# Attention and experts on one core: norms moved to ACT, bulk loads to ACT's queue, score matmuls in pairs, keys by batch

## The reference

```
x = x + attention(layernorm(x), context)     16 heads of 16, distance bias per head
x = x + experts(layernorm(x))                top 2 of 8 experts, 256 -> 1024 (gelu) -> 256
scores = q k^T / 4 - slope[h] * |key - query + 870|;  attn = softmax(scores);  out = (attn v) Wo + bo
combine = top-2 of softmax(x Wg + bg), scaled to sum 1;  y = sum_e combine[e] * (gelu(x W1[e] + b1[e]) W2[e] + b2[e])
```

## Time and profile before

| | us |
|---|---|
| median of 3 runs | 512.09 (512.02 to 512.95) |
| the profiled execution | 508.91 |
| its span | 507.1 |
| TensorE busy | 419.6 (83%) |
| VectorE busy | 312.6 (62%) |
| ACT busy | 232.4 (46%) |
| GpSimd busy | 223.7 (44%) |
| mean granted TensorE clock | 0.922 |

### The profile page before, as it was taken

One profiled execution on the slowest core, in us unless ns is written; L12 is line 12 of the kernel. 1 busy time (PEld: TensorE's weight loads), 2 busy tenths in 40 slices (PEclk: granted clock), 3 DMA queues, 4 the chain that ended last, 5 costly groups with the idle time before them and its releaser, 6 DMA issues. The chain is left out here.

```text
span 507.1 us, 16158 instructions
## 1 busy us (share of the span) xinstructions
PE 419.6 (83%) x5137; PEld 330.3 (65%) x5138; DVE 312.6 (62%) x875; ACT 232.4 (46%) x607; POOL 223.7 (44%) x305
## 2 busy tenths in 40 slices
PE   5565768897888999995179899989989998999981
PEld 2554556676666778873168677668867876777760
DVE  5357848796778777554526466636664765566560
ACT  1333636564555564563234444534543553445430
POOL 3123528887888886677602222222222232122232
PEclk9865979898989999998579999989998999999997
DMA  6574455555646535333322223113222322122110
GB/s 225 134 229 150 139 152 189 175 175 192 215 136 185 165 123 163 122 123 127 127 64 37 39 41 53 35 29 45 46 44 31 53 38 43 34 43 47 22 12 0
DMA packets 52967, 50.70 MB, mean 100 GB/s; under 512 B 22672, under 2 KB 47024, under 8 KB 52784
## 3 DMA queue, kind: packets, MB, share of 16 engines
q1 hardware_dynamic: 45192, 41.07, 27.0%
q0 software_dynamic: 7152, 8.47, 9.9%
q10 hardware_dynamic: 576, 0.53, 0.3%
HBM read 33.73 MB, written 17.50 MB: 101 GB/s over the span
## 5 line engine op out<-in xcount | busy, mean ns | idle before, releaser
L976 PE MATMUL ps<-area,wts 128*128 128x128 f16 (+1 forms) x2896 | 197.0, 243 | 0.1
L976 PEld LDWEIGHTS ps<-area,wts 128*128 (+1 forms) x2896 | 157.5, 103 | 41.0 <-issue 2.1
L976 PE MATMUL ps<-wts,area 128*128 x624 | 153.4, 330 | 2.2 <-DVE area L934 1.8
L718 ACT ACTIVATE area<-ps,late 128x128 f32<-128x128 f32 x312 | 89.2, 368 | 115.0 <-PE ps L976 115.0
L932 DVE TENSOR_SCALAR area<-area 128x512 f16<-128x512 f32 x78 | 33.0, 424 | 77.8 <-ACT area L718 77.7
L976 PE MATMUL ps<-area 128*128 128x154 f16 (+2 forms) x928 | 71.0, 236 | 12.0 <-DMA area<-qd 11.1
L976 PEld LDWEIGHTS ps<-area 128*128 128x128 f16 (+1 forms) x928 | 59.8, 107 | 21.2 <-issue 8.1
L595 POOL DMA_INDIRECT out<-o,row_id x20 | 31.6, 1579 | 95.1 <-issue 65.0
L595 POOL DMA_INDIRECT out<-xn,row_id x19 | 30.0, 1579 | 92.4 <-issue 79.8
L804 DVE TENSOR_REDUCE mx<-ps 128x3 f32<-128x462 f32 (+1 forms) x96 | 53.1, 579 | 24.3 <-PE ps L976 23.9
L621 ACT ACTIVATE area<-ps 128x512 f32<-128x512 f32 x80 | 47.3, 595 | 27.7 <-PE ps L976 25.5
(11 more groups left out here) (121 smaller groups left out, 419.1 us busy)
## 6 DMA issues: line engine op xcount, KB each, us to landing
stage<-in_w SPq DMA_DIRECT2D x32, 512.0 KB, 5.0
area<-xlist SPq DMA_DIRECT2D x39, 130.0 KB, 2.0
area<-qd SPq DMA_DIRECT2D x16, 256.0 KB, 2.7
qd<-wts SPq DMA_DIRECT2D x48, 64.0 KB, 1.9
area<-in_x SPq DMA_DIRECT2D x16, 128.0 KB, 2.3
out<-area SPq DMA_DIRECT2D x16, 128.0 KB, 1.8
xlist<-pad_rows SPq DMA_DIRECT2D x11, 130.0 KB, 2.5
area<-in_b SPq DMA_DIRECT2D x1, 1024.0 KB, 5.0
```

The lines of the kernel that those rows point to most:

```text
L718: last = nc.scalar.activation(h32[par][:, c * P:(c + 1) * P], h_ps[par][m][:, f * P:(f + 1) * P], ACT.Gelu_apprx_tanh, bias=b1T[:, ds(e * ...
L976: return nc.tensor.matmul(out_, lhsT, rhs, start=start, stop=stop, skip_group_check=skip)
```

## The change

- POOL keeps the power and gets a tiny `shift` = -mean/std. The norms themselves become one ACT instruction each, x * scale + bias. `normed2` moves from the end of turn b1 to the next turn, behind ACT's copies of xn^T and o_sb; `normed1` stands near the end of ACT's turn.
- `load_w`, `late` and the kink tables are issued by ACT, the weights at the end of its turn, and two small writes of the keys' bias rows too.
- Scores: the heads are taken in natural order, so that the two heads of a pair share one weight load and one matmul of 314 columns where both lie in one group: ten matmuls a tile instead of sixteen. The kink tiles' extra matmuls stay.
- Keys are loaded, projected, split and written batch by batch. In turns -2 and -1 the next query stands ahead of the scores. `values()` moves from turn -3 to turn -2, behind the first scores.
- One bias matmul of two rows instead of two of one. From turn 16 on VectorE's weight splits stand at the end of the turn.

The diff, cut ("..." marks what is left out):

```diff
-GROUPS = [(0, 3), (3, 3), (6, 3), (9, 3), (12, 2), (14, 2)]
+GROUPS = [(0, 3), (3, 3), (6, 2), (8, 3), (11, 3), (14, 2)]
...
-            def load_w(u):
...
                 sp.dma_start(qs[R_MAX:R_MAX + 65:64, t % 4, :, :].rearrange("p n (j t) -> p n j t", j=4), src).then_inc(S[f"m_in{t % 4}"], 16)
 
+            sp.dma_start(a_sb[:, 0:A_ONE], pack_a[:, 0:A_ONE]).then_inc(s.a_in0, 16)
             load_x(0)
-            sp.dma_start(a_sb, pack_a).then_inc(s.a_in, 16)
             sp.dma_start(c32[:], c32_in).then_inc(s.c_in, 16)
...
             for b in range(B):
+                sp.wait_ge(s.k_hi, b + 1)
+                for a in (0, 1):
+                    sp.dma_start(parts[:, a, :, b], k16[:, b, 0]).then_inc(S[f"kd_w{b}"], 16)
+                sp.wait_ge(s.k_lo, b + 1)
+                sp.dma_start(parts[:, 2, :, b], k16[:, b, 1]).then_inc(S[f"kd_w{b}"], 16)
+                if b == 0:
+                    write_q(0)
+            for b in range(B):
+                sp.wait_ge(S[f"kd_w{b}"], 80)
                 for hh in range(2):
                     cols = slice(hh * KW, hh * KW + NK)
                     sp.dma_start(kk[64 * hh:64 * hh + R_MAX, b, :, cols], kd[hh, :, :, b, :]).then_inc(S[f"kk_in{b}"], 16)
...
+            def rstd(t, mv, rs, ready, done, shifted):
+                pool.wait_ge(ready, t + 1)
...
+                pool.tensor_scalar(rs[:, 2:3], mv[:, 0:1], rs[:, 1:2], -1.0, ALU.mult, ALU.mult).then_inc(shifted, 1)
 
             def chosen(t):
...
+            def load_w(u):
+                e, second, n, place = u // 4, u % 4 // 2, u % 2, u % NSTAGE
+                wait(act, S[f"w_lo{place}"], u // NSTAGE)
+                if second:
+                    act.dma_start(staged(u), w2[e, n * 512:(n + 1) * 512, :].rearrange("(c p) d -> p c d", p=P)).then_inc(S[f"w_stage{place}"], 16)
+                else:
+                    act.dma_start(stage[:, place, :], w1[e, n * P:(n + 1) * P, :]).then_inc(S[f"w_stage{place}"], 16)
 
             def exps(t, k):
...
-                    normed(f2)
+                    turned(f2)
                 if b1 is not None:
                     act.wait_ge(s.pv_d, 4 * b1 + 4)
                     wait(act, s.otr_ps, b1)
                     nc.scalar.copy(o_sb[:], o_ps).then_inc(s.oe_d, 1)
+                if b2 is not None:
+                    normed2(b2)
...
                 if b2 is not None:
                     act.wait_ge(s.x2T_ps, b2 + 1)
                     wait(act, s.lg_ps, b2)
                     nc.scalar.copy(x2T[:], misc[:, 0:D]).then_inc(s.x2T_d, 1)
...
-
-            def normed(t):
+                for u in weight_units(i + 1) if i > -3 else []:
+                    load_w(u)
+                if i == 2:
+                    act.dma_start(kinks[:], kink_in).then_inc(s.kink_in, 16)
+                if i == -2:
+                    values()
...
+            def normed1(t):
+                act.wait_ge(s.shift1, t + 1)
+                wait(act, s.xnT_ps, t)
+                nc.scalar.activation(xn, xr[:, t % 8, :], ACT.Identity, bias=rs1[:, 2:3], scale=rs1[:, 1:2]).then_inc(s.xn_d, 1)
+
+            def normed2(t):
+                act.wait_ge(s.shift2, t + 1)
+                wait(act, s.x2T_ps, t)
+                wait(act, s.xs_lo, t)
+                nc.scalar.activation(xn2[:], xr[:, t % 8, :], ACT.Identity, bias=rs2[:, 2:3], scale=rs2[:, 1:2]).then_inc(s.xn2_d, 1)
+                act.wait_ge(s.xn2_d, t + 1)
...
-            normed(0)
-            act.wait_ge(s.k32_d, 2)
-            nc.scalar.copy(k16[:, 0], k32).then_inc(s.k_hi, 1)
-            act.wait_ge(s.kb_d, 2)
-            nc.scalar.copy(kb16[:, 0], kb32).then_inc(s.kb_hi, 1)
-            query(0)
+            normed1(0)
+            turned(0)
+            for b in range(B):
+                act.wait_ge(s.k32_d, 2 * (b + 1))
+                nc.scalar.copy(k16[:, b, 0], k32[:, b]).then_inc(s.k_hi, 1)
+                act.wait_ge(s.kb_d, b + 1)
+                nc.scalar.copy(kb16[:, b, 0], kb32[:, b]).then_inc(s.kb_hi, 1)
+                if b == 0:
+                    query(0)
+                act.wait_ge(s.kb_lo, b + 1)
+                for hh in range(2):
+                    act.dma_start(kd[hh, R_BIAS:R_MAX, :, b].rearrange("a n k -> n a k"), kb16[hh * NP:(hh + 1) * NP, b]).then_inc(S[f"kd_w{b}"], 16)
+                if b == 0:
+                    normed1(1)
+            for u in range(2):
+                load_w(u)
+            act.dma_start(late[:], pack_o).then_inc(s.o_in, 16)
...
                     positions(b2 - 1)
-                if sc is not None:
+                if -3 < i < 0:
+                    norm1(f1)
+                if sc is not None and i >= 0:
                     for g in range(3):
                         maxima(sc, g)
                 if f2 is not None and f2 > 0:
                     query_lo(f2)
+                if sc is not None and i < 0:
+                    for g in range(3):
+                        maxima(sc, g)
                 if b1 is not None:
                     dve.wait_ge(s.otr_ps, b1 + 1)
...
                     dve.transpose(nbT[:, sc % 2, :], nb16[:]).then_inc(s.nbT_d, 1)
-                if i == -3:
+                for u in earlier[1:2] + units[0:1] if i >= NT else []:
+                    split_w_lo(u)
+                if i == -2:
                     values()
                 if i == -1:
...
+            def keys_of(b):
+                pe.wait_ge(S[f"a_in{b}"], 16)
+                cols = slice(b * NK, (b + 1) * NK)
+                for hh in range(2):
+                    if b == 1:
+                        pe.wait_ge(s.k32_d, hh + 1)
+                    for c in range(DC):
+                        last = mm(ps[:, hh, cols], wk_sb[:, c, hh * P:(hh + 1) * P], ctxT[:, b, c, 0:NK], c == 0, c == 1)
...
+                    last = mm(ps[0:H, 2, cols], wkb[:, c, :], ctxT[:, b, c, 0:NK], c == 0, c == 1)
+                last.then_inc(s.kb_ps, 1)
+
+            keys_of(0)
             pe.wait_ge(s.c_in, 16)
             turn_normed(0)
             pe.wait_ge(s.wq_in, 16)
...
+                    p, hh = at_ // 2, at_ % 2
+                    both = hh == 0 and at_ + 1 < end
+                    width = KW + NK if both else NK
+                    dst = bank[:, (at_ - first) * KW:(at_ - first) * KW + width]
+                    last = mm(dst, qs[:, slot, p, :], kk[:, b, p, hh * KW:hh * KW + width], True, kink is None, True)
                     if kink is not None:
                         keys = kinks[:, kink * N_KEYS:kink * N_KEYS + NK]
-                        for m in ((0, 1), (2,))[hh]:
...
                     turn_normed(f2)
+                    if i < 0:
+                        query(f2)
                 if sc is not None:
                     for g in range(3):
                         scores(sc, g)
-                if f2 is not None and f2 > 0:
+                if f2 is not None and f2 > 0 and i >= 0:
                     query(f2)
                 if b2 is not None:
...
-                        last = mm(misc[:, D:2 * D], c16[0:1, H_SMALL:H_SMALL + P], bo_hl[:, z, :], False, z == 1)
-                    last.then_inc(s.pr_ps, 1)
+                    mm(misc[:, D:2 * D], c16[0:2, H_SMALL:H_SMALL + P], bo_hl[:], False, True).then_inc(s.pr_ps, 1)
...
                     mix(mt, 3)
-                if i == -3:
+                if i == -2:
                     values()
```

More of the change, by code:

```diff
@@ L187, in program @@
         b1T = late[:, O_B1:O_B1 + E * FC]
-        bo_row = late[0:1, O_BO:O_BO + D]
+        bo_row = late[0:2, O_BO:O_BO + D]
         area = sb("area", [P, 11616], f32)
@@ L451, in _ @@
                     read_q(0)
-            for u in range(2):
-                load_w(u)
             load_x(3)
-            sp.dma_start(late[:], pack_o).then_inc(s.o_in, 16)
             def turn(i):
@@ L842, in turn @@
                     maxima(sc, 3)
-                if f1 is not None and f1 > 0:
+                if i >= 0 and f1 is not None:
                     norm1(f1)
-                for u in earlier[1:2]:
+                for u in earlier[1:2] if i < NT else []:
                     split_w_lo(u)
@@ L848, in turn @@
                     maxima(sc, 4)
-                for u in units[0:1]:
+                for u in units[0:1] if i < NT else []:
                     split_w_lo(u)
@@ L1036, in scores @@
                 first, n = GROUPS[g]
-                for j in range(n):
-                    hh, p = (first + j) // NP, (first + j) % NP
-                    dst = ps[:, seq % 3, j * KW:j * KW + NK]
-                    last = mm(dst, qs[:, slot, p, :], kk[:, b, p, hh * KW:hh * KW + NK], True, kink is None, True)
+                end, bank = first + n, ps[:, seq % 3, :]
+                at_ = first
+                while at_ < end:
+                    p, hh = at_ // 2, at_ % 2
[3 more added lines that the diff above has]
+                    last = mm(dst, qs[:, slot, p, :], kk[:, b, p, hh * KW:hh * KW + width], True, kink is None, True)
```

(7 more changed lines are left out.)

152 lines of the change are left out of this document (65 added, 87 removed).

## The result

| us | before | after |
|---|---|---|
| median, same chip | 512.06 (4 runs) | 526.55 (4 runs) |
| ratio, 95% interval | | 1.0305 [1.0263, 1.0348] |
| the profiled execution's span | 507.1 | 525.0 |
| TensorE busy | 419.6 | 422.7 |
| mean granted clock | 0.922 | 0.902 |

The change makes the kernel 3% slower. I had forecast 488 and a range of 478 to 503: wrong in sign.

The account below looks back on a forecast made before the run. Attention turns were bound by TensorE's waits for GpSimd's norm, SP's queue and the start. Terms -4.7 - 6.8 - 9.2 - 2.6 - 0.5 = -23.8 took 508.9 to 485.1; plus 3.2 for the median, 488 us, range 478 to 503.

Parts of the forecast that it names:

- this trip: Query written to DRAM and read back: in an undisturbed turn, maxima's read issued at 6.2 us, query landing at 8.9.
- turns 0 to 2: With bulk loads off SP's queue, these turns take 9.6, 9.3 and 9.8 us, together 28.7: -6.8 us.
- the 10.4 a turn for turns 3 to 9: Norm 2 on ACT ends the wait for GpSimd; 10.4 us a turn instead of 11.86: -9.2 us with kink tables.
- The other rule of the Trainium skill: Engines alternate between queues by packets of 9 to 17 descriptors, so maxima wait a packet, not a megabyte; the sum stands.
- Rival 1: Bulk loads still slow the query's trip; 12.1 us a turn, nothing gained in turns 3 to 9: 503 us, chance 0.20.
- Rival 2: ACT's load issues at each turn's end block the copy of xn^T, 12.9 us a turn: 524 us, chance 0.06.
- Start: Up to tile 2's scores: first scores at 22.5 us, tile 2's at 39.5 instead of 44.21: -4.7 us.
- The balance of engines: Turns 3 to 9: VectorE 9.9 us, query's trip 8.9 to 9.6, ACT 10.2 at most; coupled, 10.4 a turn.
- The kink tables' price of 1.0: 944 KB issued by ACT at the end of turn 2 ahead of its next copy: 1.0 us less saved.
- The 0.2 for pairs: Ten score matmuls instead of sixteen with the same columns on TensorE: 0.2 us a turn saved, at best 0.5.
- Turns 10 to 13: TensorE full but for some 0.4 us a turn at norm 2; pairs and bias 0.3 more: -2.6 us.
- Turns 14 to 17: Norm 2 waits for the o_sb copy, +1.1; bias matmuls -0.3; turn 17's split moved, -1.3: sum -0.5 us.

Follow-up runs that it names:

- e4: The kernel before with only its bulk loads (weights, the start's loads, late, kink tables) issued by ACT at the turn's end: 1.0215 of the kernel before.
- e5: The changed kernel with weight loads from the fifth on cut to 32 of 1024 columns, part of the computation left out: 0.9773 of the kernel before.
- e2: The changed kernel, with ACT issuing a turn's bulk loads only once that turn's query read has landed: 0.9999 of the kernel before.
- e14: The changed kernel with each 512 KB weight load issued by ACT as four of 128 KB: 1.0636 of the kernel before.
- e7: The changed kernel, bulk loads back on SP behind the query's read, and SP's query writes and read ahead of the maxima's read: 0.9677 of the kernel before.
- e12: e7 with norm 2 on ACT ahead of the o_sb copy from turn 14 on: 0.9674 of the kernel before.
- e13: e9 with only the start's two weight loads and late back on SP: 0.9731 of the kernel before.
- e1: The changed kernel with weights, late and kink tables issued by SP again, behind the query's read: 0.9946 of the kernel before.
- e9: The changed kernel, loads still on ACT, with SP's query writes and read ahead of the maxima's read: 0.9807 of the kernel before.
- e10: e7 with both norms back on GpSimd: 0.9911 of the kernel before.
- e11: e7 with sixteen score matmuls a tile again instead of pairs: 0.9638 of the kernel before.

## Why the prediction was wrong

**The failed step.** "With bulk loads off SP's queue I take this trip for turns 0 to 2 as well", and the 10.4 a turn for turns 3 to 9, which has the query land at +8.9 to +9.6. The trip I took was that of an undisturbed turn. It holds if the read of the maxima never waits; I let another queue stand for that. It cost most in turns 3 to 9: 17.6 of the 41.8 us between forecast and span (+8.4 where I had -9.2), and 9.1 at the start. The runs: on ACT's queue the megabyte delays the maxima and the query's read (e4, 1.0215), without its bytes they hardly wait (e5, 0.9773; SP's waits for the maxima fall from 56.1 to 24.2 us). The sentence of the Trainium skill (DMA: Bandwidth & Descriptors, Issuing engines are not separate DMA queues) that spreading over issuing engines saves issue time only, is what the trace shows: SP waits 5.3 us at worst for maxima that stand in another queue than the loads, 5.6 before. The other rule of the Trainium skill, of turns by the packet (same page, Queues, rings and completion order), on which I let the sum stand, did not shield 8 KB here: 4.7 us in e2. Whether the rule fails, or a packet of these loads is itself long, no run shows.

**Rival 1** was this mechanism with chance 0.20 and too small a price. I gave the maxima 1.0 us more and the query's read 4.2. At 132.30 the maxima took 4.88, where the undisturbed turn 7 of before took 1.50 (128.13 to 129.63), so 3.4 more, and the read 6.5; and the price had no term for the clock that is lower behind idle stretches. My reason against it was that the bytes "no longer meet the read": they do, since the late maxima push the read behind the next turn's load.

**Rival 2** had the sign and nearly the time, but for another reason. ACT's issues take 0.33 to 0.53 each in the changed kernel's turns and run beside its running work; they block only where many stand together: 3.02 us at the start, and in e14.

**Term by term**, forecast against after, and against three of the repaired versions:

| us | forecast | after | e7 | e12 | e13 |
|---|---|---|---|---|---|
| scores of tile 2 | 39.5 | 48.58 | 40.68 | 41.98 | 43.24 |
| turns 0 to 2 | 28.7 | 30.85 | 30.46 | 30.05 | 29.15 |
| turns 3 to 9 | 73.9 | 91.46 | 76.86 | 73.03 | 73.05 |

- *Start.* The first scores at 22.5 were right once the loads are away (22.97 in e1, 22.43 in e7); ACT's loads cost them 4.7 to 5.2 us, where I had taken 0.9. values() took 6.57, not 5.5. In e1 tile 2 still came at 44.27: its query stood behind the maxima.
- *Turns 3 to 9.* The balance of engines was right: with the query out of the way a turn takes the 10.4 that I gave it (e12, e13; 10.8 in e9, 11.0 in e7). The norms did remove GpSimd's wait, ACT took 0.60 us for one and not 0.4, and TensorE waits 0.2 to 0.4 a turn for it in e12, where I had no wait. The kink tables' price of 1.0 can't be told apart. The 0.2 for pairs was 0.
- *Turns 10 to 13.* In after one read of the query kept TensorE waiting 6.34 us there. In e9 turns 10 to 12 take 34.66 us, 2.45 less than before, a little more than forecast, and by the norms alone (37.49 in e10). The pairs add nothing (e11).
- *Turns 14 to 17.* The waits for norm 2 are 1.20 three times (0.61, 0.88 and 0.63 before), +1.5 where I had +1.1, and turn 17 waits 2.90 instead of 2.47: the VectorE split that I took out of its way was not what it waited for. My -0.5, with turn 13 some -1.2, was +1.6.

What I had wrong in weight: 0.90 for faster, though the one unknown of the sum, whether a second queue helps, was shown by no row, and two rules of one page spoke on either side of it.

## What to carry to other kernels

Here a bulk transfer moved to another engine's queue still delayed the small transfers that were issued behind it. What counted in the turns was whether something urgent met it in flight, not who had issued it: with SP's new order turns 3 to 9 take 75.3 us with the loads on ACT (e9) and 76.9 with them on SP (e7). Let the transfer that the next stage waits for stand first in its issuer's program, ahead of reads that are needed a turn later, and start bulk loads right behind its read. Before splitting a gain by parts, undo each part alone: here one part (the norms) carried all of it, and could only do so once another (the queue), which more than ate it, was out of the way.

## What the runs showed that I had not expected

- SP waited up to 4.7 and 5.3 us (e2, after) for 8 KB of its own queue that met loads of ACT's, nearly as long as behind 1 MB in its own queue (5.6).
- Which came first counted: in e2 maxima issued just ahead of ACT's loads were back in 1.4 to 2.8 us, those just behind in 3.4 to 5.1.
- ACT's issues: 0.33 to 0.53 each, two of them at 140.44 while an exponential and a norm ran, without delay; but six in 3.52 us kept the next copy waiting 2.92.
- A late transfer costs the clock as well: 6.9 of the 14.6 us between the changed kernel and e7 in turns 3 to 9.
- At the start, with ACT's loads in flight, SP's issue itself stretches: 3.05 us for two reads and 2.54 for one, against 1.56 and 0.43 in e13, whose loads come behind them. Where both queues issue at once in e2, ACT's two take 1.30 (134.00) and SP's next one 1.03 (134.22).
